# The head of a mixture-of-experts kernel: loads in halves, and the second half of the tokens turned by VectorE

## The chip, the cores and the metric

One NeuronCore of a Trainium2 chip runs the kernel. The metric is the device time of one execution in microseconds (us). All times below are in us, counted in the trace from the start of the profiled span.

## The reference

The input x has 8 sequences of 128 tokens, D = 128. Eight routed experts and one shared expert, each with F = 512, are applied to all tokens; nothing is skipped, the gates only weigh.

```
g = einsum('bsd,edf->ebsf', x, Wg);  u = einsum('bsd,edf->ebsf', x, Wu)      # E = 8
expert_outs   = einsum('ebsf,efd->ebsd', silu(g) * u, Wd)
expert_output = einsum('be,ebsd->bsd', gates, expert_outs)                   # gates: fside_Bx8_0
shared        = einsum('bsf,fd->bsd', silu(x @ Sg) * (x @ Su), Sd)
out = x + (1 - sg) * expert_output + sg * shared                             # sg: one number per sequence
```

## The kernel before, in words

**Layout.** The 1024 tokens are two halves of N = 512. A half is held transposed, features on the 128 partitions and tokens in the free dimension (`x_t`), in an order in which token 4p + q of the half is column 128q + p. A "unit" is one slice of 128 of the 512 hidden features of one expert for one half: 4 slices x 2 halves = 8 units per expert, 72 in all. All matmuls run in FP32R on values that are split in a high part (the rounded copy, `hi`) and the rest (`lo = whole - hi`); a product takes three matmuls (hi x hi, hi x lo, lo x hi) of 128x128 weights against 512 columns. A unit is nine matmuls: three for the gate (`g_ps`), three for up (`u_ps`), three for down (`y_ps`), the down ones two units late (LAG = 2).

**What follows a unit's matmuls.** ScalarE takes silu of g_ps (`silu_of`), VectorE multiplies it with u_ps into a bank of PSUM (`hidden`, L380), ScalarE makes the high part of that (`hidden_hi`, L303), VectorE the low part (`hidden_lo`, L385); then TensorE can do the down matmuls of the unit, that with h_lo last (L464). Two banks each for g, u and h: unit k's gate matmuls wait for silu k-2, its up matmuls for product k-2. Each engine runs its own list of instructions strictly in order; what stands behind a waiting instruction on its engine waits too. `.then_inc` and `wait_ge` are the semaphores between them.

**The head.** SyncE's queue issues, in this order: x first half, Sg, Su, x second half, Sd, the shared gate broadcast to 128 partitions, the gates broadcast to 128 partitions, then Wg, Wu, Wd of routed expert 1. TensorE does warm-up matmuls on zeros until the first half of x is there, and transposes it (L472). ScalarE and VectorE split it and the first weights (`first_hi`, L357, L273), VectorE and GpSimd the low parts. Then TensorE does the gate and up matmuls of the first two units (L483 to L502), turns the second half of x (four transposes, L508) and goes on to the units 3 to 8 of the shared expert (L519 to L529). VectorE does, in order: split of GATE 0:2, x_lo of the first half (L367), split of UP 2:4, split of DOWN (L357), products one and two (L380), first h_lo (L385), x_lo of the second half (L398), `not_sg` (L401) and `coef` = gates x (1 - sg) (L405), and from then on product, h_lo, product, h_lo. ScalarE takes the high part of the second half of x (L285) between the first and the second `hidden_hi`.

**Preparing the routed experts.** For each of them GpSimd scales x by coef (`xs`, L237; before the first expert it also adds hi and lo back to `x_t`, L224), ScalarE and GpSimd split xs and the weights, slice by slice, between their other work; for expert 1 ScalarE's first slice (L293) comes behind the third silu and needs all three of that expert's loads. Routed experts run in loops of the same pattern until a tail of transposes and stores that the change doesn't touch. In that tail the first half's result is turned by VectorE in 32x32 blocks (L432) and stored by four DMAs of 64 KB in rows of 128 B (L190).

Of the kernel before, what the change touches and what calls it, by code (L numbers as in the profile page):

```python
# [8 lines left out]
ALU = mybir.AluOpType  # L9
# [11 lines left out]
WARM_UP = 5  # L21


def build(nc, x, gates, shared_gate, Wg, Wu, Wd, Sg, Su, Sd, out):
# [21 lines left out]
    with ctx:  # L46
# [6 lines left out]
        x_nat = sbuf("x_nat", [P, HALVES, NQ, D], FP32)  # L53
# [41 lines left out]
        x_loaded = [sem(f"x_loaded{h}") for h in range(HALVES)]  # L95
        sg_loaded = sem("sg_loaded")
        gates_loaded = sem("gates_loaded")
        first_w_loaded = [sem(f"first_w_loaded{k}") for k in range(3)]
# [4 lines left out]
        one_minus = sem("one_minus")  # L103
        coef_ready = sem("coef_ready")
# [3 lines left out]
        x_t_done = sem("x_t_done")  # L108
        first_act_hi = sem("first_act_hi")
# [46 lines left out]

        @block.sync
        def _(sp):
            sp.dma_start(x_nat[:, 0, :, :], x_view[0]).then_inc(x_loaded[0], DMA)
            sp.dma_start(w_raw[0][:, GATE, :, :], in_slices(Sg)).then_inc(first_w_loaded[GATE], DMA)  # L160
            sp.dma_start(w_raw[0][:, UP, :, :], in_slices(Su)).then_inc(first_w_loaded[UP], DMA)
            sp.dma_start(x_nat[:, 1, :, :], x_view[1]).then_inc(x_loaded[1], DMA)
            sp.dma_start(w_raw[0][:, DOWN, :, :], in_rows(Sd)).then_inc(first_w_loaded[DOWN], DMA)
# [6 lines left out]
            sp.dma_start(sg_sb[:, :], shared_gate.partition_broadcast(P)).then_inc(sg_loaded, DMA)  # L170
            sp.dma_start(gates_sb[:, :, :], gates.partition_broadcast(P)).then_inc(gates_loaded, DMA)
# [28 lines left out]
        def _(pool):  # L200
# [19 lines left out]
            def whole_tokens(h):  # L220

                pool.wait_ge(x_hi_done, h + 2)
                pool.wait_ge(x_lo_done, h + 2)
                pool.tensor_tensor(x_t[:, h, :], f32(x_hi[:, h, :]), f32(x_lo[:, h, :]), ALU.add)\  # L224
                    .then_inc(x_t_done, 1)

            def prepare(e, buf, halves_before, slices_before, first=False):
                for h in range(HALVES):
                    if first:
                        whole_tokens(h)  # L230
                        pool.wait_ge(x_t_done, h + 1)
# [35 lines left out]
        def _(act):  # L267
            act.wait_ge(zeros_set, 1)
            act.activation(table[:, :], zeros[:, 0:1], ACT.Silu)

            def first_hi(k, n, m):
                act.wait_ge(first_w_loaded[k], DMA)
                act.activation(w_hi[0][:, k, n:m, :], w_raw[0][:, k, n:m, :], ACT.Copy)\  # L273
                   .then_inc(first_act_hi, 1)

            for i in range(2):
                act.wait_ge(x_transposed, i + 1)
                act.activation(x_hi[:, 0, i * HALF_N:(i + 1) * HALF_N], first_ps[i][:, 0:HALF_N], ACT.Copy)\
                   .then_inc(x_hi_done, 1)
# [73 lines left out]
        def _(dve):  # L353
            dve.memset(zeros[:, :], 0.0).then_inc(zeros_set, 1)

            def first_hi(k, n, m):
                dve.tensor_copy(w_hi[0][:, k, n:m, :], w_raw[0][:, k, n:m, :]).then_inc(first_dve_hi, 1)  # L357

            dve.wait_ge(first_w_loaded[GATE], DMA)
# [3 lines left out]
                              f32(w_hi[0][:, GATE, 0:2, :]), ALU.subtract).then_inc(first_dve_lo, 1)  # L363
            for i in range(2):
# [80 lines left out]
        def _(pe):  # L445
            def warm(cols):
                pe.matmul(u_ps[1][:, 0:cols], zeros[:, 0:P], zeros[:, 0:cols], start=True, stop=True)
# [21 lines left out]
            pe.wait_ge(x_loaded[0], DMA)  # L469
            for i in range(2):  # L470
                for q in range(HALF_Q):
                    last = pe.transpose(first_ps[i][:, q * P:(q + 1) * P], x_nat[:, 0, i * HALF_Q + q, :],  # L472
                                        ident[:, :])
                last.then_inc(x_transposed, 1)
            warm(HALF_N)
# [9 lines left out]
            pe.wait_ge(first_dve_lo, 1)  # L485
            for f in range(BANKS):
                pe.matmul(g_ps[f][:, :], w_lo[0][:, GATE, f, :], x_hi[:, 0, :], start=False, stop=False,
                          skip_group_check=True)
# [4 lines left out]
            pe.wait_ge(first_act_hi, 2)  # L493
# [6 lines left out]
            pe.wait_ge(first_pool_lo, 2)  # L500
# [3 lines left out]


            pe.wait_ge(x_loaded[1], DMA)
            for q in range(NQ):
                last = pe.transpose(y_ps[1][:, q * P:(q + 1) * P], x_nat[:, 1, q, :], ident[:, :])  # L508
            last.then_inc(x_transposed, 1)

            for k in range(BANKS, UNITS):
                f, h = k % NF, k // NF
                g, u = g_ps[k % BANKS], u_ps[k % BANKS]
                if k == NF:
                    pe.wait_ge(x_hi_done, 3)
                    pe.wait_ge(x_lo_done, 3)
                pe.wait_ge(silu_done, k - BANKS + 1)
                pe.wait_ge(first_act_hi, 1)
                pe.matmul(g[:, :], w_hi[0][:, GATE, f, :], x_hi[:, h, :], start=True, stop=False)  # L519
                pe.matmul(g[:, :], w_hi[0][:, GATE, f, :], x_lo[:, h, :], start=False, stop=False)  # L520
                pe.wait_ge(first_pool_lo, 1)
                pe.matmul(g[:, :], w_lo[0][:, GATE, f, :], x_hi[:, h, :], start=False, stop=True)\  # L522
# [9 lines left out]
                pe.wait_ge(first_pool_lo, 4 if k == BANKS else 5)  # L532
                down(k - LAG, k - LAG, 0, begin=(k - LAG) % NF == 0)
# [82 lines left out]
```

## Time and profile before

| | us |
|---|---|
| median of three runs (lowest, highest) | 158.86 (158.67, 158.95) |
| the profiled execution's own time | 158.84 |
| its span, first to last instruction | 157.0 |
| TensorE busy | 153.0 |
| VectorE, ScalarE, GpSimd busy | 99.2, 108.2, 78.5 |
| ScalarE: table load ends, first x_hi starts, first silu starts | 2.03, 4.26, 6.74 |
| GpSimd: first sum x_t, first xs start | 11.37, 12.75 |
| TensorE: the four transposes of the second half of x | 8.13 to 8.48 |

Busy time of TensorE is modelled: a matmul of 512 columns shows 0.389 us, but the next one starts 0.227 later, so starts are what one should subtract. "DMA" in the chain means that an instruction waited for a transfer.

### The profile page before, as it was taken

Reading aid. Unit: us, or ns where it says so; the run is one execution under the profiler, and the core shown is the slowest. Engines: PE = TensorE matmul, PEld = TensorE weight load, DVE = VectorE, ACT = ScalarE, POOL = GpSimd, SP = SyncE. Lnnn points to the kernel's source line nnn. Section 1 sums busy time; section 2 is a strip of 40 time slices with the busy share of each in tenths; the row PEclk is TensorE's granted clock in tenths of the full one; section 3 lists DMA queues with packets and bytes.
Section 4 is the critical chain, followed back from the end, with each engine's and each line's share of the span. In section 5 each row is a group of like instructions: output and inputs, shape, how many; then the busy total and the mean of one; then the engine's idle time right before and its main releaser. Section 6 shows DMA issues by size and latency. Waiting matters only on the chain.

```text
span 157.0 us, 2316 instructions
## 1 busy us (share of the span) xinstructions
PE 153.0 (97%) x674; PEld 124.8 (79%) x674; DVE 99.2 (63%) x160; ACT 108.2 (69%) x200; POOL 78.5 (50%) x79
## 2 busy tenths in 40 slices
PE   6999999999999999999999999999999999999992
PEld 2886888888888888888888888888888888888872
DVE  0695767766666666666666666666665666666782
ACT  3658767877577757775887667766776688755531
POOL 1549993556455464547255825573547354650000
DMA  5584014003300140006000600060000000000005
GB/s 157 187 265 136 0 49 156 0 0 104 100 0 0 39 168 0 0 14 186 0 0 0 200 0 0 0 199 1 0 0 0 0 0 0 0 0 4 0 10 124
DMA packets 10326, 8.24 MB, mean 52 GB/s; under 512 B 2896, under 2 KB 7760, under 8 KB 10320
## 3 DMA queue, kind: packets, MB, share of 16 engines
q1 hardware_dynamic: 10176, 8.03, 17.0%
q10 hardware_dynamic: 144, 0.13, 0.3%
q8 instruction: 3, 0.05, 0.1%
q14 instruction: 3, 0.02, 0.0%
HBM read 7.64 MB, written 0.52 MB: 52 GB/s over the span
## 4 chain that ended last, share of the span: by engine, by line
PE 89%; DMA 4%; SPq 2%; ACT 1%; DVE 1%; issue 0%
PE y_ps L464 10%; PE y_ps L461 10%; PE y_ps L459 10%; PE u_ps L551 9%; PE g_ps L546 9%; PE g_ps L547 9%; PE u_ps L552 9%; PE u_ps L550 9%; PE g_ps L545 9%; DMA w_raw<-in_L_cond_Wd 4%; DVE h_ps L380 0%; PE g_ps L520 0%; PE u_ps L526 0%; PE u_ps L527 0%; PE g_ps L522 0%; PE g_ps L519 0%
## 5 line engine op out<-in xcount | busy, mean ns | idle before, releaser
L380 DVE TENSOR_TENSOR h_ps<-silu,u_ps 128x512 f32<-128x512 f32 x71 | 49.4, 696 | 49.0 <-PE u_ps L552 45.6
L303 ACT ACTIVATE h_hi<-h_ps 128x512 fp32r<-128x512 f32 x71 | 42.6, 600 | 38.8 <-DVE h_ps L380 38.8
L242 POOL TENSOR_TENSOR w_lo<-w_raw,w_hi 128x384 fp32r<-128x384 f32 x32 | 32.5, 1019 | 37.7 <-ACT w_hi L293 37.7
L385 DVE TENSOR_TENSOR h_lo<-h_ps,h_hi 128x512 fp32r<-128x512 f32 x71 | 48.5, 683 | 0.1
L298 ACT ACTIVATE silu<-g_ps 128x512 f32<-128x512 f32 x72 | 42.9, 597 | 0.4 <-PE g_ps L491 0.4
L247 POOL TENSOR_TENSOR xs_lo<-xs,xs_hi 128x512 fp32r<-128x512 f32 x16 | 20.7, 1292 | 16.1 <-ACT xs_hi L289 16.1
L464 PE MATMUL y_ps<-h_lo,w_hi 128*128 128x512 f32 x71 | 27.9, 392 | 0.1
L459 PE MATMUL y_ps<-h_hi,w_lo 128*128 128x512 f32 x71 | 27.6, 389 | 0.0
L461 PE MATMUL y_ps<-h_hi,w_hi 128*128 128x512 f32 x71 | 27.6, 389 | 0.0
L545 PE MATMUL g_ps<-x_hi,w_hi 128*128 128x512 f32 x64 | 24.9, 389 | 0.0
L546 PE MATMUL g_ps<-x_lo,w_hi 128*128 128x512 f32 x64 | 24.9, 389 | 0.0
L547 PE MATMUL g_ps<-x_hi,w_lo 128*128 128x512 f32 x64 | 24.9, 389 | 0.0
L550 PE MATMUL u_ps<-xs_hi,w_hi 128*128 128x512 f32 x64 | 24.9, 389 | 0.0
L551 PE MATMUL u_ps<-xs_lo,w_hi 128*128 128x512 f32 x64 | 24.9, 389 | 0.0
L552 PE MATMUL u_ps<-xs_hi,w_lo 128*128 128x512 f32 x64 | 24.9, 389 | 0.0
L293 ACT ACTIVATE w_hi<-w_raw 128x384 fp32r<-128x384 f32 x32 | 16.6, 517 | 1.1 <-DMA w_raw<-in_L_cond_Wd 1.1
L237 POOL TENSOR_TENSOR xs<-x_t,coef 128x512 f32<-128x512 f32 x16 | 16.4, 1045 | 0.2
L464 PEld LDWEIGHTS y_ps<-h_lo,w_hi 128*128 128x128 f32 x71 | 13.3, 188 | 3.6 <-DVE h_lo L385 0.8
L459 PEld LDWEIGHTS y_ps<-h_hi,w_lo 128*128 128x128 f32 x71 | 13.3, 188 | 2.8
L461 PEld LDWEIGHTS y_ps<-h_hi,w_hi 128*128 128x128 f32 x71 | 13.3, 188 | 2.8
L545 PEld LDWEIGHTS g_ps<-x_hi,w_hi 128*128 128x128 f32 x64 | 12.0, 188 | 2.5
L550 PEld LDWEIGHTS u_ps<-xs_hi,w_hi 128*128 128x128 f32 x64 | 12.0, 188 | 2.5
(80 smaller groups left out, 119.8 us busy)
## 6 DMA issues: line engine op xcount, KB each, us to landing
w_raw<-in_L_cond_Wg SPq DMA_DIRECT2D x8, 256.0 KB, 2.7
w_raw<-in_L_cond_Wu SPq DMA_DIRECT2D x8, 256.0 KB, 3.1
w_raw<-in_L_cond_Wd SPq DMA_DIRECT2D x8, 256.0 KB, 3.6
x_nat<-in_x SPq DMA_DIRECT2D x2, 256.0 KB, 3.5
w_raw<-in_L_cond_Sg SPq DMA_DIRECT2D x1, 256.0 KB, 2.8
w_raw<-in_L_cond_Su SPq DMA_DIRECT2D x1, 256.0 KB, 4.2
w_raw<-in_L_cond_Sd SPq DMA_DIRECT2D x1, 256.0 KB, 4.7
out<-y_blk SPq DMA_DIRECT2D x4, 64.0 KB, 2.2
```

The lines of the kernel that those rows point to most:

```text
L298: act.activation(silu[k % BANKS][:, :], g_ps[k % BANKS][:, :], ACT.Silu)\
L303: act.activation(h_hi[k % HB][:, :], h_ps[k % BANKS][:, :], ACT.Copy)\
L380: dve.tensor_tensor((to or h_ps[k % BANKS])[:, :], silu[k % BANKS][:, :], u_ps[k % BANKS][:, :], ALU.mult).then_inc(hidden_done, 1)
L385: dve.tensor_tensor(h_lo[k % HB][:, :], h_ps[k % BANKS][:, :], f32(h_hi[k % HB][:, :]), ALU.subtract).then_inc(h_lo_done, 1)
L459: pe.matmul(y_ps[h][:, :], lo, h_hi[k % HB][:, :], start=begin, stop=False, skip_group_check=True)
L461: pe.matmul(y_ps[h][:, :], hi, h_hi[k % HB][:, :], start=False, stop=False, skip_group_check=True)
L464: pe.matmul(y_ps[h][:, :], hi, h_lo[k % HB][:, :], start=False, stop=f == NF - 1, skip_group_check=True)\
L545: pe.matmul(g[:, :], hi, x_hi[:, h, :], start=True, stop=False)
L546: pe.matmul(g[:, :], hi, x_lo[:, h, :], start=False, stop=False)
L547: pe.matmul(g[:, :], lo, x_hi[:, h, :], start=False, stop=True).then_inc(gate_done, 1)
L550: pe.matmul(u[:, :], hi, xs_hi[buf][:, h, :], start=True, stop=False)
L551: pe.matmul(u[:, :], hi, xs_lo[buf][:, h, :], start=False, stop=False)
```

## The change

- The loads of x's first half, Sg and Su are each split in two; UP's first half is split and multiplied before GATE's second half on ScalarE and GpSimd.
- The shared gate and the gates are loaded to one partition, by ScalarE's queue; VectorE computes one row of 72 coefficients there, TensorE spreads it to 128 partitions with a matmul against ones, VectorE copies it to `coef`.
- The second half of x is no longer loaded in rows of 2 KB and transposed by TensorE. It comes in four loads of 64 KB, each of 512 rows of 128 B, two issued by ScalarE's queue, two by SyncE's behind Sd; VectorE turns it in 32x32 blocks with one instruction ahead of the first product, into `x_t`, which the high part (ScalarE) and the low part (now GpSimd) are taken from.
- `x_t` of the first half is copied from PSUM by ScalarE, ahead of its first silu.
- Gate matmuls of the later units use w_lo before x_lo. Fewer warm-up matmuls at the start, three of 256 columns between the two halves of the first transposes.

The diff, cut to its core:

```diff
--- before.py
+++ after.py
@@ constants
-WARM_UP = 5
+WARM_UP = 4
+WARM_BETWEEN = 3
@@ tensors
-        x_nat = sbuf("x_nat", [P, HALVES, NQ, D], FP32)
+        x_nat = sbuf("x_nat", [P, NQ, D], FP32)
+        x_blk = sbuf("x_blk", [P, N], FP32)
...
-        gates_sb = sbuf("gates_sb", [P, B, E], FP32)
-        sg_sb = sbuf("sg_sb", [P, B], FP32)
-        not_sg = sbuf("not_sg", [P, B], FP32)
-        coef = sbuf("coef", [P, E, B], FP32)
+        gates_row = sbuf("gates_row", [1, B, E], FP32)
+        not_sg = sbuf("not_sg", [1, B], FP32)
+        row = sbuf("row", [1, E + 1, B], FP32)
+        ones = sbuf("ones", [1, P], FP32)
+        coef = sbuf("coef", [P, E + 1, B], FP32)
-        zeros = sbuf("zeros", [P, N], BF16)
+        zeros = sbuf("zeros", [P, P], BF16)
@@ loads
+        def load_blocks(queue, c):
+            of = x_view[1][:, :, c * BLK:(c + 1) * BLK].rearrange("(s j) q d -> j q s d", j=BLK)
+            queue.dma_start(x_blk[c * BLK:(c + 1) * BLK, :].rearrange("j (q s d) -> j q s d", q=NQ, d=BLK), of)\
+                 .then_inc(second_x_loaded, DMA)
@@ SyncE
-            sp.dma_start(x_nat[:, 0, :, :], x_view[0]).then_inc(x_loaded[0], DMA)
-            sp.dma_start(w_raw[0][:, GATE, :, :], in_slices(Sg)).then_inc(first_w_loaded[GATE], DMA)
-            sp.dma_start(w_raw[0][:, UP, :, :], in_slices(Su)).then_inc(first_w_loaded[UP], DMA)
-            sp.dma_start(x_nat[:, 1, :, :], x_view[1]).then_inc(x_loaded[1], DMA)
-            sp.dma_start(w_raw[0][:, DOWN, :, :], in_rows(Sd)).then_inc(first_w_loaded[DOWN], DMA)
+            load_tokens(0)
+            load_slices(GATE, Sg, 0)
+            load_tokens(1)
+            load_slices(GATE, Sg, 1)
+            load_slices(UP, Su, 0)
+            load_slices(UP, Su, 1)
+            sp.dma_start(w_raw[0][:, DOWN, :, :], in_rows(Sd)).then_inc(first_down_loaded, DMA)
+            load_blocks(sp, 2)
+            load_blocks(sp, 3)
...
-            sp.dma_start(sg_sb[:, :], shared_gate.partition_broadcast(P)).then_inc(sg_loaded, DMA)
-            sp.dma_start(gates_sb[:, :, :], gates.partition_broadcast(P)).then_inc(gates_loaded, DMA)
@@ GpSimd
             pool.wait_ge(first_act_hi, 1)
+            first_lo(UP, 0, 2)
+            pool.wait_ge(first_act_hi, 2)
             first_lo(GATE, 2, 4)
-            pool.wait_ge(first_act_hi, 2)
-            first_lo(UP, 0, 2)
...
-            def whole_tokens(h):
...
+            def second_x_lo():
+                pool.wait_ge(x1_hi_done, 1)
+                pool.tensor_tensor(x_lo[:, 1, :], x_t[:, 1, :], f32(x_hi[:, 1, :]), ALU.subtract)\
+                    .then_inc(x1_lo_done, 1)
@@ ScalarE
+            act.dma_start(row[:, E, :], shared_gate.partition_broadcast(1)).then_inc(sg_loaded, DMA)
+            act.dma_start(gates_row[:, :, :], gates.partition_broadcast(1)).then_inc(gates_loaded, DMA)
             act.wait_ge(zeros_set, 1)
             act.activation(table[:, :], zeros[:, 0:1], ACT.Silu)
+            load_blocks(act, 0)
+            load_blocks(act, 1)
...
+            def first_x_t(i):
+                act.wait_ge(x_lo_done, i + 1)
+                act.activation(x_t[:, 0, i * HALF_N:(i + 1) * HALF_N], first_ps[i][:, 0:HALF_N], ACT.Copy)\
+                   .then_inc(x_t_done, 1)
+            first_hi(UP, 0, 2)
             first_hi(GATE, 2, 4)
-            first_hi(UP, 0, 2)
+            first_x_t(0)
+            first_x_t(1)
             def second_x_hi():
-                act.wait_ge(x_transposed, 3)
-                act.activation(x_hi[:, 1, :], y_ps[1][:, :], ACT.Copy).then_inc(x_hi_done, 1)
+                act.wait_ge(x1_turned, 1)
+                act.activation(x_hi[:, 1, :], x_t[:, 1, :], ACT.Copy).then_inc(x1_hi_done, 1)
...
+            second_x_hi()
             hidden_hi(0, 0)
-            second_x_hi()
             hidden_hi(1, 1)
@@ VectorE
+            dve.memset(ones[:, :], 1.0).then_inc(ones_set, 1)
+            dve.wait_ge(sg_loaded, DMA)
+            dve.tensor_scalar(not_sg[:, :], row[:, E, :], -1.0, 1.0, ALU.mult, ALU.add)\
+               .then_inc(one_minus, 1)
...
+            dve.wait_ge(gates_loaded, DMA)
+            dve.wait_ge(one_minus, 1)
+            dve.tensor_tensor(row[:, 0:E, :].rearrange("p e b -> p b e"), gates_row[:, :, :],
+                              not_sg[:, :].unsqueeze(2).to_broadcast([1, B, E]), ALU.mult)\
+               .then_inc(row_ready, 1)
...
+            dve.wait_ge(row_spread, 1)
+            dve.tensor_copy(coef[:, :, :], y_ps[1][:, 0:(E + 1) * B].rearrange("p (e b) -> p e b", b=B))\
+               .then_inc(coef_ready, 1)
             first_hi(DOWN, 0, 4)
...
+            dve.wait_ge(second_x_loaded, DMA * (P // BLK))
+            dve.transpose(x_t[:, 1, :], x_blk[:, :]).then_inc(x1_turned, 1)
+            dve.wait_ge(x_t_done, 2)
             hidden(0, 0, first=True)
             hidden(1, 1, first=True)
             hidden_lo(0, 0)
-            dve.wait_ge(x_hi_done, 3)
-            dve.tensor_tensor(x_lo[:, 1, :], y_ps[1][:, :], f32(x_hi[:, 1, :]), ALU.subtract)\
-               .then_inc(x_lo_done, 1)
...
@@ TensorE
             for i in range(2):
+                pe.wait_ge(first_x_loaded[i], DMA)
...
-            warm(HALF_N)
+                if i == 0:
+                    for _ in range(WARM_BETWEEN):
+                        warm(HALF_N)
...
+            pe.wait_ge(ones_set, 1)
+            pe.wait_ge(row_ready, 1)
+            pe.matmul(y_ps[1][:, 0:(E + 1) * B], ones[:, :], row[:, :, :].rearrange("p e b -> p (e b)"), start=True,
+                      stop=True).then_inc(row_spread, 1)
...
-            pe.wait_ge(x_loaded[1], DMA)
-            for q in range(NQ):
-                last = pe.transpose(y_ps[1][:, q * P:(q + 1) * P], x_nat[:, 1, q, :], ident[:, :])
-            last.then_inc(x_transposed, 1)
```

## Rows read from the trace of the kernel before

**Rows 1.** The page: busy us (share of the span) and instructions of each engine.

```profile
PE 153.0 (97%) x674; PEld 124.8 (79%) x674; DVE 99.2 (63%) x160; ACT 108.2 (69%) x200; POOL 78.5 (50%) x79
```

**Rows 2.** Timeline (start, duration, engine, line, operation; idle before and releaser), TensorE.

```profile
12.53 0.19 PEld L464 LDWEIGHTS y_ps<-h_lo,w_hi 128*128 128x128 f32 x1 [0.30 <-DVE h_lo L385]
...
14.92 0.19 PEld L464 LDWEIGHTS y_ps<-h_lo,w_hi 128*128 128x128 f32 x1 [0.49 <-DVE h_lo L385]
...
15.26 0.39 PE L519 MATMUL g_ps<-x_hi,w_hi 128*128 128x512 f32 x1
...
149.92 0.39 PE L545 MATMUL g_ps<-x_hi,w_hi 128*128 128x512 f32 x1
```

**Rows 3.** Chain of waits in order of time (start, duration, what).

```profile
12.04 0.53 ACT w_hi L293
```

**Rows 4.** Timeline, VectorE in the head.

```profile
7.33 0.75 DVE L357 CAST w_hi<-w_raw 128x512 fp32r<-128x512 f32 x1 [1.00 <-DMA w_raw<-in_L_cond_Sd]
...
8.18 1.29 DVE L380 TENSOR_TENSOR h_ps<-silu,u_ps 128x512 f32<-128x512 f32 x2
...
10.14 0.68 DVE L398 TENSOR_TENSOR x_lo<-y_ps,x_hi 128x512 fp32r<-128x512 f32 x1
...
11.01 0.28 DVE L405 TENSOR_TENSOR coef<-gates_sb,not_sg 128x64 f32<-128x64 f32 x1
...
11.15 0.73 DVE L380 TENSOR_TENSOR h_ps<-silu,u_ps 128x512 f32<-128x512 f32 x1
```

**Rows 5.** Timeline, VectorE's turn of the result in the tail.

```profile
150.70 0.70 DVE L432 STREAM_TRANSPOSE y_blk<-y_t 128x512 f32<-128x512 f32 x1
...
151.33 0.65 DVE L385 TENSOR_TENSOR h_lo<-h_ps,h_hi 128x512 fp32r<-128x512 f32 x1
```

**Rows 6.** Timeline, ScalarE in the head.

```profile
8.91 0.60 ACT L303 ACTIVATE h_hi<-h_ps 128x512 fp32r<-128x512 f32 x1 [1.08 <-DVE h_ps L380]
...
9.40 0.59 ACT L285 ACTIVATE x_hi<-y_ps 128x512 fp32r<-128x512 f32 x1
```

**Rows 7.** Timeline, SyncE's first issues.

```profile
1.21 0.42 SPq L160 DMA_DIRECT2D w_raw<-in_L_cond_Sg  x1
...
1.66 0.43 SPq L161 DMA_DIRECT2D w_raw<-in_L_cond_Su  x1
...
2.14 0.43 SPq L162 DMA_DIRECT2D x_nat<-in_x  x1
```

**Rows 8.** DMA issues of 1.5 to 3.5: size each, us from issue to landing.

```profile
w_raw<-in_L_cond_Sg SPq DMA_DIRECT2D x1, 256.0 KB, 2.8
w_raw<-in_L_cond_Su SPq DMA_DIRECT2D x1, 256.0 KB, 4.2
x_nat<-in_x SPq DMA_DIRECT2D x1, 256.0 KB, 4.4
w_raw<-in_L_cond_Sd SPq DMA_DIRECT2D x1, 256.0 KB, 4.7
```

**Rows 9.** DMA rate from 0 to 20, forty steps of 0.5.

```profile
GB/s 0 0 0 57 233 324 377 287 242 264 326 313 136 76 20 77 216 279 366 334 237 143 301 339 367 335 185 10 0 0 0 0 0 0 0 0 0 0 0 0
```

**Rows 10.** The tail: line 190's issues, DMA rate 153 to 154, SyncE's last store.

```profile
L190 SPq DMA_DIRECT2D out<-y_blk x4: 614/629/705, 151.4 to 153.5; - x4
...
DMA to landing us min/median/max: 2.2/2.2/2.3
...
GB/s 148 148 123 113 154 143 138 133 139 118 123 82 32 15 0 0 0 0 46 67 82 118 143 138 148 138 143 148 138 143 108 148 154 128 138 128 123 123 77 32
...
154.23 0.58 SPq L193 DMA_DIRECT2D out<-out_sb  x1
```

**Rows 11.** Timeline, TensorE's start: warm-up weight loads, one per matmul; first gate matmuls.

```profile
2.03 0.15 PEld L447 LDWEIGHTS u_ps<-zeros 128*128 128x128 bf16 x1 [0.28 <-issue]
...
2.45 0.15 PEld L447 LDWEIGHTS u_ps<-zeros 128*128 128x128 bf16 x1 [0.28 <-issue]
...
4.79 1.20 PE L483 MATMUL g_ps<-x_hi,w_hi 128*128 128x256 f32 x4
```

More of the change, by code:

```diff
@@ L93, in build @@
         nat_ps = [g_ps[1], u_ps[0], y_ps[0]]
-        x_loaded = [sem(f"x_loaded{h}") for h in range(HALVES)]
+        first_x_loaded = [sem(f"first_x_loaded{i}") for i in range(2)]
+        second_x_loaded = sem("second_x_loaded")
         sg_loaded = sem("sg_loaded")
         gates_loaded = sem("gates_loaded")
-        first_w_loaded = [sem(f"first_w_loaded{k}") for k in range(3)]
+        first_w_loaded = [[sem(f"first_w_loaded{k}_{i}") for i in range(2)] for k in (GATE, UP)]
+        first_down_loaded = sem("first_down_loaded")
         w_loaded = [sem(f"w_loaded{i}") for i in range(2)]
@@ L103, in build @@
         one_minus = sem("one_minus")
+        ones_set = sem("ones_set")
+        row_ready = sem("row_ready")
+        row_spread = sem("row_spread")
         coef_ready = sem("coef_ready")
@@ L108, in build @@
         x_t_done = sem("x_t_done")
+        x1_turned = sem("x1_turned")
+        x1_hi_done = sem("x1_hi_done")
+        x1_lo_done = sem("x1_lo_done")
         first_act_hi = sem("first_act_hi")
@@ L229, in prepare @@
                     if first:
[L230 to L231 removed]
+                        if h == 1:
+                            second_x_lo()
+                        pool.wait_ge(x_t_done, 2)
                     else:
@@ L354, in _ @@
             dve.memset(zeros[:, :], 0.0).then_inc(zeros_set, 1)
+            dve.memset(ones[:, :], 1.0).then_inc(ones_set, 1)
+            dve.wait_ge(sg_loaded, DMA)
+            dve.tensor_scalar(not_sg[:, :], row[:, E, :], -1.0, 1.0, ALU.mult, ALU.add)\
+               .then_inc(one_minus, 1)
             def first_hi(k, n, m):
                 dve.tensor_copy(w_hi[0][:, k, n:m, :], w_raw[0][:, k, n:m, :]).then_inc(first_dve_hi, 1)
-            dve.wait_ge(first_w_loaded[GATE], DMA)
+            dve.wait_ge(first_w_loaded[GATE][0], DMA)
             first_hi(GATE, 0, 2)
@@ L446, in warm @@
             def warm(cols):
-                pe.matmul(u_ps[1][:, 0:cols], zeros[:, 0:P], zeros[:, 0:cols], start=True, stop=True)
+                pe.matmul(u_ps[1][:, 0:cols], zeros[:, :],
+                          zeros[:, :].unsqueeze(1).to_broadcast([P, cols // P, P]), start=True, stop=True)
             pe.wait_ge(zeros_set, 1)
@@ L484, in _ @@
                               stop=False, skip_group_check=True)
[L485 to L488, printed above, removed]
+                pe.wait_ge(first_dve_lo, 1)
+                for f in range(BANKS):
+                    pe.matmul(g_ps[f][:, cols], w_lo[0][:, GATE, f, :], x_hi[:, 0, cols], start=False,
+                              stop=False, skip_group_check=True)
+            pe.wait_ge(ones_set, 1)
+            pe.wait_ge(row_ready, 1)
+            pe.matmul(y_ps[1][:, 0:(E + 1) * B], ones[:, :], row[:, :, :].rearrange("p e b -> p (e b)"), start=True,
+                      stop=True).then_inc(row_spread, 1)
             pe.wait_ge(x_lo_done, 2)
@@ L514, in _ @@
                 if k == NF:
-                    pe.wait_ge(x_hi_done, 3)
-                    pe.wait_ge(x_lo_done, 3)
+                    pe.wait_ge(x1_hi_done, 1)
                 pe.wait_ge(silu_done, k - BANKS + 1)
-                pe.wait_ge(first_act_hi, 1)
+                pe.wait_ge(first_act_hi, 2)
                 pe.matmul(g[:, :], w_hi[0][:, GATE, f, :], x_hi[:, h, :], start=True, stop=False)
-                pe.matmul(g[:, :], w_hi[0][:, GATE, f, :], x_lo[:, h, :], start=False, stop=False)
-                pe.wait_ge(first_pool_lo, 1)
-                pe.matmul(g[:, :], w_lo[0][:, GATE, f, :], x_hi[:, h, :], start=False, stop=True)\
+                pe.wait_ge(first_pool_lo, 2)
+                pe.matmul(g[:, :], w_lo[0][:, GATE, f, :], x_hi[:, h, :], start=False, stop=False)
+                if k == NF:
+                    pe.wait_ge(x1_lo_done, 1)
+                pe.matmul(g[:, :], w_hi[0][:, GATE, f, :], x_lo[:, h, :], start=False, stop=True)\
                   .then_inc(gate_done, 1)
```

37 lines of the change are left out of this document (17 added, 20 removed).

## The prediction

> **What bounds the kernel now.** The page first: TensorE is busy for 153.0 of 157.0 us [rows 1]. Then how even its stream is: the first gate matmul of the shared expert's sixth unit starts at 15.26, that of the last unit of all (66 units later) at 149.92, so a unit takes 134.66 / 66 = 2.040 us, nine matmuls at 0.227 [rows 2]. That leaves no stall behind 15.26 that this change could touch, and the tail is not edited. What the change does to the time is by how much it moves that 15.26.
>
> The chain of waits says what sets 15.26: ScalarE's first split of routed expert 1 starts at 12.04, when its last weights (Wd) have landed, and h_hi, silu, product and h_lo follow, up to the matmul that takes h_lo at 14.92 [rows 2, 3]. So one bound is the landing T of that Wd, plus 15.26 - 12.04 = 3.22. The timeline of VectorE shows the second: its split of the down weights starts at 7.33, when Sd lands, the first product of silu and up at 8.18, and, behind the first h_lo, x_lo of the second half and two gate operations fill 10.14 to 11.15, ahead of the third product [rows 4]. TensorE waits for h_lo twice: 0.3 us before 12.53, and 0.49 before 14.92, and the next gate matmul behind such a wait comes 0.34 later instead of 0.227 [rows 2].
>
> **The chain that the new order makes.** I call L the moment at which VectorE starts to turn the second half. The turn of 128x512 stands in the trace once, at 150.70, and what follows it at 151.33: 0.63 [rows 5]. First product at L+0.63, second at L+1.28 (the two took 1.29 together [rows 4]). ScalarE's h_hi starts 0.03 behind a product's end and takes 0.60: L+1.36 to 1.95. First h_lo L+1.98 to 2.66, TensorE's matmul on it at L+2.70; the fourth unit starts 0.34 later, at L+3.04. ScalarE goes at 0.48 from one instruction to the next [rows 6]: second h_hi L+1.96, third silu L+2.44 to 3.04. With x_lo and the gate operations gone from here, the third product runs L+3.08 to 3.78 and the second h_lo L+3.68 to 4.36. TensorE wants it at L+3.04 + 8 x 0.227 = L+4.86, so there is no stall; the fifth unit starts at L+5.09, wants the third h_lo at L+6.91 and has it at L+6.2; the sixth unit starts at L+7.13. Checked on the kernel before: its first product at 8.18 means L = 7.55, a fourth unit at 10.59 (the trace has 10.65) and a sixth at 14.68; the 0.58 up to 15.26 are mostly the two stalls. So the new sixth unit starts at the later of L + 7.13 and T + 3.22, and the change is even where L is 8.13: it gives back 0.58 and pays for whatever puts the first product behind 8.18.
>
> **What sets L.** VectorE must have done the split of the down weights (0.65 behind the landing of Sd, if the turn follows at the pitch of rows 5, 0.75 at most by its duration [rows 4]), and all four block loads must have landed.
>
> Issues. SP's stand 0.45 to 0.48 apart, 0.47 on average [rows 7]. After the change Sd is the seventh, at 0.75 + 6 x 0.47 = 3.6, SP's two blocks come at 4.0 and, because a transfer of 512 short rows took 0.61 to 0.71 to issue in the tail [rows 10], at 4.7, done by 5.3. Sg had 2.8 from issue to landing, the blocks of the tail 2.2 [rows 8, 10], so the issues alone would allow Sd at 6.4 and the blocks at 6.9. The queue's data decide, not the issues.
>
> Data. The rate climbs from 57 GB/s at 1.5 to 324 at 2.5 and stays at 240 to 380 until 6.0 [rows 9]. Summed, 1024 KB are through by 5.4 and 1211 KB by 6.0. Last byte and landing stand 0.4 to 1.3 apart: Sg is 512 KB, reached at 3.6, landed 1.21 + 2.8 = 4.0; Su 768 KB, 4.55, landed 1.66 + 4.2 = 5.86; x of the second half 1024 KB, 5.4, landed 2.14 + 4.4 = 6.5 [rows 7 to 9]. Ahead of and with Sd there will be 1024 KB again (x's first half, Sg, Su, Sd), but beside them ScalarE's two blocks of 512 rows of 128 B. What such a load costs the trace doesn't show; its nearest row is the store of the same blocks in the tail, where busy engines moved 138 to 148 GB/s [rows 10]: 64 KB in 0.44 us. The cheap bound is the rate of long rows, 330 GB/s, 0.20 us. The dear bound: the broadcasts of the two gate tensors, 256 rows of 32 and 256 B, hold the queue from 6.2 to 7.6 at rates down to 20 GB/s [rows 9], 1.4 us for 16 rows on each of 16 DMA engines, 88 ns a row; at that price all 2048 rows would take 11 us. The blocks read distinct addresses, as those of the tail, so I take 0.44 each.
>
> Then Sd has its last byte at 5.4 + 2 x 0.44 = 6.3 and lands between 6.7 and 7.6, mean 7.15: VectorE is free at 7.8. SP's blocks have theirs at 6.3 + 0.88 = 7.15 and land between 7.55 and 8.45, mean 8.0. L = 8.0, set by the blocks. At the cheap rate Sd lands at 5.4 + 0.4 + 0.85 = 6.65 and the blocks at 7.05: L = 7.3, set by the split; with the late end of both landings L = 8.45.
>
> Forecast: sixth unit at 8.0 + 7.13 = 15.13, 0.13 earlier. T: 768 KB behind the blocks at 330 GB/s end at 7.15 + 2.33 = 9.5, with 1.4 to landing 10.9 (before: from 7.6, through near 10.6, landed at 12.04); the issues, the last at 6.3, would allow less. T + 3.22 = 14.1 is not the bound: the 1.1 us that the removed broadcasts give to Wd is bought and not used.
>
> The Trainium skill, "DMA: Bandwidth & Descriptors", section "Why small descriptors are slow (HBM only)", puts a fixed 3 cycles beside the 32 B beats of each packet; at its 850 MHz that makes an estimate of 8.2 ns for 128 B, 0.26 us a block where the tail's row says 0.44. By the page L would be about 7.45 and the time 158.2, by the row 158.7. The trace does not agree for stores (138 to 148 GB/s where that rule gives 248) and shows no such load, so the row is kept.
>
> **Edits costed at nothing, and what covers them.**
> - Loads in halves, UP's first half ahead of GATE's second: the first half of x can land by 0.75 + 2.2 = 2.95, x_hi starts 0.7 behind. The gate matmuls then start near 4.2 instead of 4.79 [rows 11], still at the slow pitch of rows 11 (0.42 for 512 columns, 1.2 GHz; 0.227 is 2.4 GHz). They end at 6.1 to 6.6, the up ones at 7.5 to 8.0, the third unit's gate ones by 8.7: all before the first product ends, at L+1.36 = 9.4. TensorE gains 0.1 to 0.6 and hands it to that wait; queued behind it are the third unit's up matmuls and the first down, which are in the chain above.
> - Four transposes less on TensorE (0.35), one matmul on a single row more: same cover.
> - ScalarE: two gate issues (0.9) ahead of the table load, which then ends at 2.9 instead of 2.03, two block issues (1.3) beside or behind it, 4.5 at worst; gates done as now even then. Two copies x_t of 0.38 ahead of the first silu, which comes by 7.5 instead of 6.74; it is needed, done, at 8.6.
> - VectorE: the row product on one partition, before 4.7, in its wait for x_hi; the copy of coef (nearest: the gate product, 0.28 [rows 4]) between up and down split, free unless Su's second half lands after 6.9; then 0.1.
> - GpSimd: two sums x_t less, x_lo of the second half more, 1.30 each; it is ready by 12 and TensorE wants it at L+5.5 = 13.5.
>
> **Sum.** The profiled execution took 158.84 for its span of 157.0, the median of three is 158.86: one and the same. 158.84 - 0.13 = 158.7.
>
> **Rivals.**
> 1. The blocks are cheap and the split of the down weights decides: L = 7.3 to 7.7, time 158.84 - 0.83 to - 0.43, say 158.2. For it: up to 377 GB/s on long rows, and Sg landed only 0.4 behind its last byte. Against: the stores of the tail.
> 2. The other side: the block loads land late, and VectorE, whose products all stand behind them in order, holds the kernel; each 0.1 us of landing past 8.13 is 0.1 lost. Issues of SP and ScalarE that take turns at one generator of descriptors would do it: 2 x 0.45 + 2 x 0.63 = 2.2 us of ScalarE's between SP's bring the last block's issue to 6.9, its landing, by 2.2, to 9.1: 158.84 + 0.97 = 159.8. For it: SP's last store, beside ScalarE's, took 0.58 to issue where loads of as many rows take 0.43 [rows 10]. Against: nothing else in the trace has two queues at once. Short rows at twice the tail's price give L = 5.4 + 3.5 + 0.85 = 9.75 and 160.5, at the broadcasts' price 165 or more.
> 3. TensorE, waiting 0.8 us near 9, falls back to the pitch of 0.42: some 15 matmuls at 0.2 more each, 3 us, 161.8. No wait of the kernel before is over 0.5 once it has sped up, so the trace bears it neither out nor down.
> 4. It does not do what it says: T comes at 12.04 again and binds; the sixth unit stays at 15.26. 158.85.
>
> **Chances.** Forecast 0.42 (own range 158.4 to 159.1), rival 1 0.26, rival 2 0.24, rival 3 0.03, rival 4 0.05. 0.2% is 0.32 us, about what a measurement of this kernel can tell from no change. Faster by more: rival 1 and a third of the forecast's range, 0.40. Slower: rivals 2 and 3 and a tenth of the forecast, 0.31. Within: 0.29. The range reaches from L = 7.3 to L = 9.4 (rival 2 without its dearest prices): 158.0 to 160.1.
>
> **What would show it.** Right: the turn starts at 7.8 to 8.3, at once behind the last block's landing; the first product 0.63 later; no wait for h_lo after 11; the sixth unit at 15.0 to 15.3, and 2.040 a unit behind it; Wd of expert 1 lands before 11; the stretch of idle DMA near 7 is gone. Wrong: block loads at another price than 0.44 each (SP's pair against Sd), SP's issues further apart than 0.47 while ScalarE issues, a pitch of 0.42 after 9, or a sixth unit later than L + 7.13, which would be a wait that I missed.

## The result, and the profile after

The changed kernel takes 159.45 us (159.13 to 160.03), the kernel before, timed beside it, 158.90 (158.46 to 159.40): a ratio of 1.0033, interval 1.0020 to 1.0045. It is slower, by 0.5 us, where 158.7, a little faster, was forecast. The profiled execution took 159.45 for a span of 157.6.

The timeline of TensorE answers to [rows 2]: the fourth, fifth and sixth unit, and the last.

```profile
11.86 0.39 PE L571 MATMUL g_ps<-x_hi,w_hi 128*128 128x512 f32 x1
...
13.94 0.39 PE L571 MATMUL g_ps<-x_hi,w_hi 128*128 128x512 f32 x1
...
15.98 0.39 PE L571 MATMUL g_ps<-x_hi,w_hi 128*128 128x512 f32 x1
...
150.62 0.39 PE L605 MATMUL g_ps<-x_hi,w_hi 128*128 128x512 f32 x1
```

The sixth unit stands at 15.98 instead of 15.26, and (150.62 - 15.98) / 66 = 2.040 a unit follow, as before. The loss, 0.72, is in the head; the profiled executions differ by 0.61, since the tail here takes 0.1 less. This holds for all fourteen profiled executions of this document: the time is the start of the sixth unit plus 143.47 to 143.58. So a time without a profile can be read as an estimate of its sixth unit: time - 143.5.

VectorE's timeline answers to [rows 4], with the turn that stood in the tail alone in [rows 5]:

```profile
7.71 0.76 DVE L405 CAST w_hi<-w_raw 128x512 fp32r<-128x512 f32 x1 [0.68 <-DMA w_raw<-in_L_cond_Sd]
8.81 0.71 DVE L451 STREAM_TRANSPOSE x_t<-x_blk 128x512 f32<-128x512 f32 x1 [0.34 <-DMA x_blk<-in_x]
9.44 1.26 DVE L436 TENSOR_TENSOR h_ps<-silu,u_ps 128x512 f32<-128x512 f32 x2
10.77 0.69 DVE L441 TENSOR_TENSOR h_lo<-h_ps,h_hi 128x512 fp32r<-128x512 f32 x1
11.86 0.70 DVE L436 TENSOR_TENSOR h_ps<-silu,u_ps 128x512 f32<-128x512 f32 x1 [0.39 <-ACT silu L342]
```

L, the moment at which VectorE starts to turn the second half, is 8.81, and the chain of the prediction puts the sixth unit at 8.81 + 7.13 = 15.94. Sd landed at 7.71 (before: 7.33), the last block only as the turn started, and the first product, 0.63 behind, comes 1.26 later than before; 0.58 of it is given back by the two stalls that are gone. TensorE waits for that product once, and goes on at its old pace of 0.23:

```profile
10.16 0.50 PE L580 MATMUL u_ps<-x_hi,w_hi 128*128 128x512 f32 x1 [0.94 <-DVE h_ps L436]
10.50 0.39 PE L581 MATMUL u_ps<-x_lo,w_hi 128*128 128x512 f32 x1
```

SyncE's and ScalarE's issues, and what the queue moved (the row of [rows 9] again, steps of 0.5):

```profile
1.66 1.36 ACTq L175 DMA_DIRECT2D x_blk<-in_x  x2
...
2.63 1.13 SPq L186 DMA_DIRECT2D w_raw<-in_L_cond_Su  x2
...
3.81 0.43 SPq L194 DMA_DIRECT2D w_raw<-in_L_cond_Sd  x1
...
4.28 1.41 SPq L175 DMA_DIRECT2D x_blk<-in_x  x2
```

```profile
GB/s 0 0 0 53 263 215 224 227 263 320 240 183 289 225 113 259 245 285 363 280 138 12 0 115 295 352 190 332 272 16 0 0 0 0 0 0 0 0 0 0
```

By 6.0 it has moved 994 KB (the sum of the steps, halved) where before it had 1211. Most of the difference, 161 of 217 KB, arises from 2.5 to 4.0: 215, 224 and 227 GB/s where the kernel before had 324, 377 and 287. The second bound, T + 3.22 (T is the landing of Wd of expert 1), is out of the way: ScalarE's first split of expert 1 starts with no wait.

```profile
11.71 0.53 ACT L337 ACTIVATE w_hi<-w_raw 128x384 fp32r<-128x384 f32 x1
```

### The profile page after: what moved, and what is told of

The parts are those of the page before. It is cut to its first block, busy times and chain, and to the rows that moved or that the text cites. A ratio compares the mean times of both kernels' runs of the same rounds, so it can differ in the third digit from the quotient of the medians.

```text
span 157.6 us, 2328 instructions
## 1 busy us (share of the span) xinstructions
PE 152.8 (97%) x675; PEld 124.2 (79%) x675; DVE 99.3 (63%) x162; ACT 109.1 (69%) x202; POOL 77.3 (49%) x78
## 4 chain that ended last, share of the span: by engine, by line
PE 92%; SPq 3%; DMA 2%; issue 1%; DVE 0%; ACT 0%; DVEq 0%
PE y_ps L514 10%; PE y_ps L511 10%; PE y_ps L509 10%; PE u_ps L611 9%; PE u_ps L610 9%; PE g_ps L606 9%; PE g_ps L605 9%; PE u_ps L612 9%; PE g_ps L607 9%; DMA x_blk<-in_x 2%; SPq L186 1%; PE u_ps L580 1%; PE u_ps L583 1%; PE u_ps L581 1%; PE g_ps L573 1%; PE g_ps L576 1%
## 5 line engine op out<-in xcount | busy, mean ns | idle before, releaser
L607 PEld LDWEIGHTS g_ps<-x_hi,w_lo 128*128 128x128 f32 x64 | 12.0, 188 | 2.5
```

Of the source, the lines that this page charges most:

```text
L607: pe.matmul(g[:, :], lo, x_hi[:, h, :], start=False, stop=True).then_inc(gate_done, 1)
```

## Experiments

Theory A: the place of the turn is the loss. Theory B: the loads in halves and the blocks delay what VectorE waits for. Later, for what delays the loads: theory C says that the halves slow the queue, rival D that it is ScalarE's two block loads ahead of Sd. Each result is the median, then its ratio to the kernel before on the same chip with the interval. The diffs are cut to their core, some calls shortened. One execution of each kernel was profiled, and it need not stand for the median.

**1. The turn behind the first h_lo.**

```diff
-dve.wait_ge(second_x_loaded, ...); dve.transpose(x_t[:, 1, :], x_blk[:, :])
 hidden(0, 0, first=True); hidden(1, 1, first=True); hidden_lo(0, 0)
+dve.wait_ge(second_x_loaded, ...); dve.transpose(x_t[:, 1, :], x_blk[:, :])
-second_x_hi()            # ScalarE, ahead of hidden_hi(0)
+second_x_hi()            # ScalarE, behind silu_of(2)
```

> The changed kernel with one thing moved: VectorE turns the second half behind the first h_lo instead of ahead of the first product, and ScalarE takes its high part behind the third silu. Loads and all else as changed. Theory A (the turn's place: all products stand behind the last block's landing, and the sixth unit of the changed kernel is L + 7.13 with L = 8.81): the first product now waits only for the split of the down weights, from 8.81 + 0.63 = 9.44 back to 7.71 + 0.70 = 8.4; the turn runs near 10.4, the third product waits for it until 11.0, the third h_lo is ready at 14.4 and wanted at 14.7, the sixth unit starts at 14.9 to 15.0 instead of 15.98: about 158.4 to 158.5 where the changed kernel takes 159.45. Theory B (the loads in halves and the blocks on the queues delay Su and Sd, the place is indifferent): the first product stays behind 9 and the time within 0.3 of the changed kernel.

158.71, 0.9988 (0.9970 to 1.0006): 0.45% below the changed kernel, whose interval it doesn't touch. VectorE:

```profile
7.76 0.54 DVE L406 CAST w_hi<-w_raw 128x512 fp32r<-128x512 f32 x1 [0.20 <-DMA w_raw<-in_L_cond_Sd]
8.41 1.29 DVE L437 TENSOR_TENSOR h_ps<-silu,u_ps 128x512 f32<-128x512 f32 x2
9.78 0.69 DVE L442 TENSOR_TENSOR h_lo<-h_ps,h_hi 128x512 fp32r<-128x512 f32 x1
10.38 0.70 DVE L456 STREAM_TRANSPOSE x_t<-x_blk 128x512 f32<-128x512 f32 x1
11.01 0.67 DVE L437 TENSOR_TENSOR h_ps<-silu,u_ps 128x512 f32<-128x512 f32 x1
```

The loads are as late as in the changed kernel, but the first product is 1.03 earlier and the sixth unit stands at 15.01. Theory A holds. The forecast of 158.4 to 158.5 is met by the profiled execution (158.48), and missed by the median.

**2. Block loads with long rows.** The same bytes, 4 rows of 512 B to a partition; the tokens of the second half are then not in their places.

```diff
-of = x_view[1][:, :, c * BLK:(c + 1) * BLK].rearrange("(s j) q d -> j q s d", j=BLK)
+of = x_view[1][c * BLK:(c + 1) * BLK, :, :]
```

> The changed kernel with its four block loads reading long rows: the same four transfers of 64 KB to the same 32 partitions each, but 4 rows of 512 B to a partition instead of 16 rows of 128 B (what is turned is then not the second half's tokens in their right places). Theory A with the price of short rows as the mis-sized term: SyncE issues them 0.47 apart instead of 0.70, they take 0.2 instead of 0.44 or more of the queue each, Sd lands at 7.1 to 7.3 instead of 7.71 and the last block at 7.7 or before instead of 8.79; the turn then waits for the split of the down weights and starts at 7.8 to 8.0, sixth unit at 15.0 to 15.1, time 158.5 to 158.6. Rival (not the rows but the number of transfers and bytes ahead of them sets L): last block at 8.4 or later, time 159.1 or more.

Its times scatter from 159.3 to 161.9, so only its trace (159.28) is read. The issues are shorter, but Sd still lands at 7.79, and the turn now waits for the split and not for a block:

```profile
7.79 0.93 DVE L405 CAST w_hi<-w_raw 128x512 fp32r<-128x512 f32 x1 [1.14 <-DMA w_raw<-in_L_cond_Sd]
8.64 0.70 DVE L451 STREAM_TRANSPOSE x_t<-x_blk 128x512 f32<-128x512 f32 x1
```

SyncE's blocks took 3.1 from issue to landing, so the last was there near 8.0, some 0.8 before that of the changed kernel (8.79; I had worked out 4 x 0.24 = 0.96, and 0.2 of the 0.8 is an earlier issue). Sd, behind ScalarE's two blocks, gained nothing from their long rows, where the price of 0.44 instead of 0.20 for each would have given it 0.5. So short rows don't explain Sd, and their price isn't settled by this run. Sixth unit 15.78, and 8.64 + 7.13 = 15.77. The forecast of L near 8.0 missed.

**3. The first part alone** (halves, gate rows; the second half in 2 KB rows and through TensorE, as before).

```diff
-load_blocks(sp, 2); load_blocks(sp, 3)      # and both of ScalarE
+sp.dma_start(x_nat1[:, :, :], x_view[1])    # ahead of Sd
-dve.transpose(x_t[:, 1, :], x_blk[:, :])   # x_lo by VectorE behind the first h_lo, as before
...
+for q in range(NQ): pe.transpose(y_ps[1][:, q * P:(q + 1) * P], x_nat1[:, q, :], ident[:, :])
```

> Only the first part of the change: x's first half, Sg and Su in halves, gate rows on one partition and spread by TensorE, x_t of the first half by ScalarE. The second half comes as before in rows of 2 KB ahead of Sd, is transposed by TensorE, split by ScalarE and VectorE where the kernel before has it. Theory A (only the turned second half costs): first product at 8.2 to 8.4, no gate operations between x_lo and the third product, Wd of expert 1 landed by 11, the sixth unit at 14.7 to 14.9 instead of 15.26 before: 158.3 to 158.5, the 0.5 of stalls of before won. Theory B (halves and gate rows cost, since SyncE issues two transfers more ahead of Sd): Su and Sd land 0.3 to 0.5 later than before, first product at 8.6 or later, time equal to before or slower.

158.76, 0.9987 (0.9974 to 1.0000). This is B's side: the time is not told from that of before, Sd landed at 7.93, 0.6 later than before, and the first product started at 8.87, 0.69 later. A's 158.4 missed. What the product waited for were not the loads, though, but the up matmuls:

```profile
8.87 1.29 DVE L428 TENSOR_TENSOR h_ps<-silu,u_ps 128x512 f32<-128x512 f32 x2 [0.51 <-PE u_ps L553]
```

**4. The gate rows alone**, all loads whole and in their old order (the diff is against the kernel before).

```diff
-sp.dma_start(sg_sb[:, :], shared_gate.partition_broadcast(P)); sp.dma_start(gates_sb[:, :, :], ...)
+act.dma_start(row[:, E, :], shared_gate.partition_broadcast(1)); act.dma_start(gates_row[:, :, :], ...)
+pe.matmul(y_ps[1][:, 0:(E + 1) * B], ones[:, :], row, start=True, stop=True)
...                                                     # row product and copy of coef by VectorE
```

> The kernel before with the gate tensors alone changed: both loaded to one partition by ScalarE's queue, row of 72 coefficients spread by one matmul and copied by VectorE. All other loads whole and in their old order. Both theories: the dead stretch of the DMA queue from 6.2 to 7.6 goes and Wd of expert 1 lands at 10.5 to 10.9 instead of 12.0; the two gate operations leave the place between x_lo and the third product. By the two bounds the sixth unit is at 7.55 + 7.13 = 14.7 to 14.8: 158.3 to 158.4. If instead the landing of Wd stays near 12, the broadcasts were not what held the queue, and the time stays within 0.1 of before.

158.78, 0.9988 (0.9969 to 1.0007). The dead stretch of the queue is gone, as forecast, and it has moved 1233 KB by 6.0; the time is not the 158.3 to 158.4 forecast. TensorE says why, in the head:

```profile
6.17 0.44 PE L500 MATMUL y_ps<-row,ones 1*128 1x72 f32 x2
6.54 0.73 PE L504 MATMUL g_ps<-x_lo,w_hi 128*128 128x512 f32 x2
7.11 0.62 PE L508 MATMUL u_ps<-x_hi,w_hi 128*128 128x512 f32 x2
```

The spread matmul, on one row and 72 columns, holds TensorE for 0.37; what it delays are the up matmuls that the first product waits for (8.53 instead of 8.18). I had costed it at nothing. In experiment 3 the same 0.37 is about half of the 0.69; the other half is not accounted for.

**5. The changed kernel with whole loads** of x's first half, Sg and Su.

```diff
-load_tokens(0); load_slices(GATE, Sg, 0); load_tokens(1); load_slices(GATE, Sg, 1)
-load_slices(UP, Su, 0); load_slices(UP, Su, 1)
+sp.dma_start(x_nat[:, :, :], x_view[0])               # warm-up matmuls as in the kernel before
+sp.dma_start(w_raw[0][:, GATE, :, :], in_slices(Sg)); sp.dma_start(w_raw[0][:, UP, :, :], in_slices(Su))
```

> The changed kernel with x's first half, Sg and Su loaded whole again (three transfers of 256 KB instead of six of 128 KB, warm-up matmuls as before); blocks, gate rows and the turn's place as changed. Theory C (the halves slow the queue: 994 KB through by 6.0 in the changed kernel, 1021 with long block rows, 995 in the kernel without blocks, against 1211 before and 1233 with gate rows alone): 1150 KB or more by 6.0, Sd lands at 7.0 to 7.3 instead of 7.71, the last block 0.6 to 0.9 earlier, 7.9 to 8.2, so L = 7.9 to 8.2 and the sixth unit at 15.0 to 15.4 instead of 15.98: 158.7 to 158.9. Rival D (ScalarE's blocks ahead of Sd are what slows it): Sd stays at 7.6 or later, L at 8.6 or later, 159.3 or more.

159.28, 1.0018 (0.9997 to 1.0038). The interval overlaps that of the changed kernel (1.0020 to 1.0045), so in time no gain is shown, and the median is rival D's side. The profiled execution has C's side, but it is the third fastest of twelve (158.76):

```profile
7.22 0.74 DVE L394 CAST w_hi<-w_raw 128x512 fp32r<-128x512 f32 x1 [0.43 <-DMA w_raw<-in_L_cond_Sd]
8.07 0.71 DVE L440 STREAM_TRANSPOSE x_t<-x_blk 128x512 f32<-128x512 f32 x1
```

```profile
GB/s 0 0 0 33 70 377 406 324 303 188 287 291 235 296 330 342 350 278 84 3 0 4 135 287 389 337 333 81 7 0 0 0 0 0 0 0 0 0 0 0
```

1140 KB by 6.0; L = 8.07, sixth unit 15.24 (8.07 + 7.13 = 15.20). The median of 159.28 stands for a sixth unit near 15.78, so an L near 8.65, against the 8.81 of the changed kernel, whose profiled execution took the median time. These two are estimates by time - 143.5 and L + 7.13.

**6. All blocks by SyncE, behind Sd**, loads in halves.

```diff
-load_blocks(act, 0); load_blocks(act, 1)
+load_blocks(sp, 0); load_blocks(sp, 1)     # ahead of load_blocks(sp, 2)
```

> The changed kernel with all four block loads issued by SyncE behind Sd, none by ScalarE; loads still in halves. Rival D (ScalarE's two blocks, 128 KB ahead of Sd, and their issues beside SyncE's, delay Sd): Su's second half is issued at 3.1 and Sd at 3.56 instead of 3.81, Sd lands at 7.0 to 7.2. Theory C (halves): Sd gains 0.2 from the issue and some 0.3 from the bytes at most, 7.3 or later. By both the last block lands later than 8.79, since SyncE needs 2 x 0.68 us more to issue: at 9.4 to 9.8; the chain is L + 7.13, so 16.5 to 16.9 and 160.0 to 160.4.

159.79, 1.0057 (1.0036 to 1.0078), 0.2 below its forecast. Sd landed early, at 6.84, as rival D has it, and VectorE waited longer for the blocks:

```profile
6.84 0.82 DVE L405 CAST w_hi<-w_raw 128x512 fp32r<-128x512 f32 x1 [0.25 <-DMA w_raw<-in_L_cond_Sd]
8.96 0.71 DVE L451 STREAM_TRANSPOSE x_t<-x_blk 128x512 f32<-128x512 f32 x1 [1.30 <-DMA x_blk<-in_x]
```

Sixth unit 16.12 (8.96 + 7.13 = 16.09). Here and in the changed kernel the last block sets L, in 2 and 5 the split of the down weights; the last block was 0.5 earlier than I expected. Rival D is not shown by the early Sd: in experiment 9, with the same issues, Sd landed at 7.71.

**7 and 8. Late turn with whole loads; then the spread matmul behind the first up matmuls too**, its copy behind the turn. 7 is the edits of 1 and 5; 8 adds:

```diff
-pe.matmul(y_ps[1][:, 0:(E + 1) * B], ones, row, ...)    # ahead of w_hi GATE x x_lo
 up matmuls of the units 1 and 2
+pe.matmul(y_ps[1][:, 0:(E + 1) * B], ones, row, ...)
-dve.tensor_copy(coef, y_ps[1])                          # ahead of the split of DOWN
 dve.transpose(x_t[:, 1, :], x_blk[:, :])
+dve.tensor_copy(coef, y_ps[1])
```

> Turn behind the first h_lo and whole loads together, spread matmul where the change has it, between the two halves of the gate matmuls. By the sum of both: Sd at 7.1 to 7.3, so VectorE could start the first product at 8.0; but the gate matmuls start at 4.8 as before and the spread matmul holds TensorE 0.37 us (6.07 to 6.44 in the changed kernel), so the up matmuls end at 8.5 and the first product starts there, as it did at 8.53 with gate rows alone: sixth unit at 15.0 to 15.1, 158.5 to 158.6. If the spread matmul costs nothing, first product at 8.0 to 8.2 and 158.2.

> As the one with the turn behind the first h_lo and whole loads, and the spread matmul moved behind the up matmuls of the first two units, its copy to coef behind the turn. TensorE then ends the first up product at 8.15 as before, first product 8.15 to 8.2; the spread takes its 0.37 where the four transposes stood (0.35). L' = 8.18 - 0.63 = 7.55, fourth unit at 10.6, the copy (0.15 to 0.23) delays the third product to 11.0 and the second h_lo to 12.3, wanted at 12.4; sixth unit at 14.7 to 14.8: 158.3, 0.3% below the kernel before. If the copy and the turn together are too much for VectorE, a wait for h_lo of 0.1 to 0.3 appears near 12.4 or 14.5 and the time is that of the kernel with the spread in place.

158.88, 1.0006 (0.9988 to 1.0024), and 159.01, 1.0006 (0.9991 to 1.0021): both medians missed. The profiled execution of 7, its fastest (158.50, sixth unit 14.99), is as forecast; Sd landed at 7.62 and the first product started at 8.41. With whole loads the late turn is thus no faster than with halves (158.71 in experiment 1). In 8 the first product started at 8.49, still behind the up matmuls, and coef came late (copy at 11.08). GpSimd's program has its first xs, which needs coef, ahead of x_lo of the second half; that x_lo ended at 13.65 and TensorE waited 0.40 for it: the sixth unit stands at 15.42. A copy moved out of one wait went into another.

```profile
11.36 1.04 POOL L257 TENSOR_TENSOR xs<-x_t,coef 128x512 f32<-128x512 f32 x1 [1.22 <-DVE coef L444]
12.36 1.29 POOL L242 TENSOR_TENSOR x_lo<-x_t,x_hi 128x512 fp32r<-128x512 f32 x1
```

**9 to 12. Late turn put together with the rest.** 9: all blocks by SyncE. 10: as 9, the spread matmul behind the up matmuls, its copy ahead of the turn. 11: as 10, two of the blocks by ScalarE between its first copies. 12: as 10, whole loads.

```diff
 hidden_lo(0, 0)
+dve.tensor_copy(coef, y_ps[1])                          # 10, 11, 12
 dve.transpose(x_t[:, 1, :], x_blk[:, :])
 act.activation(x_hi[:, 0, ...], first_ps[i][:, 0:HALF_N], ACT.Copy)
+load_blocks(act, i)                                     # 11 alone
```

> The changed kernel with two things moved: the turn behind the first h_lo, and all four block loads issued by SyncE behind Sd. With the blocks behind, Sd landed at 6.84 instead of 7.71 and the up matmuls ended at 8.2; with the turn late, nothing of VectorE's head waits for the blocks, which landed at 8.96 there and are wanted at 10.0. First product at 8.2, where the up matmuls end, L' = 7.57, sixth unit at 14.7 to 14.8; the landing T of Wd of expert 1, issued at 8.0 with 3.6 to 4.0 to go, 11.6 to 12.0, gives T + 3.22 = 14.8 to 15.2 as the second bound: 158.3 to 158.7. Should T not bind, 158.3; if the time is that of the late turn alone (158.7), T or the up matmuls took over.

> As the one with the turn late and all blocks by SyncE behind Sd, and the spread matmul moved behind the first up matmuls, its copy between the first h_lo and the turn. The up matmuls end 0.37 earlier, 7.83; the split of the down weights at 7.6; first product 7.85, L' = 7.2, so 14.4 by the first bound, but T + 3.22 stays at 14.8 to 15.2 by the second: 158.3 to 158.7, no better than with the spread in place. If it is 158.0, T was not what held it.

> As the one before it, but two blocks issued by ScalarE between its first copies x_hi (at 3.8 and 4.9, behind most of the shared expert's bytes), two by SyncE behind Sd. SyncE then issues Wd of expert 1 at 6.7 to 6.9, T at 10.7 to 11.2, T + 3.22 at 14.4 at most; Sd lands at 7.0 to 7.3, first product at 7.9 to 8.1, sixth unit at 14.5 to 14.7: 158.0 to 158.3, below both kernels. If ScalarE's issues (0.66 each) delay its x_hi of the second quarter or its split of the up weights by more than 0.3, the up matmuls end at 8.3 and it is 158.5.

> The kernel with the turn late, four block loads by SyncE behind Sd and the spread matmul behind the up matmuls (158.48, the best so far), now with x's first half, Sg and Su loaded whole. If the halves cost the queue what the sums by 6.0 say (922 to 1045 KB in all eight kernels with halves, 1126 to 1233 in the five with whole loads), Sd lands at 7.2 to 7.4 instead of 7.77 and the sum by 6.0 is over 1120 KB; but the first gate weights then land at 4.2 instead of 3.4 and TensorE ends its up matmuls of the first unit near 8.3, which takes the place of the split as what the first product waits for: first product 8.3 to 8.5, sixth unit 14.9 to 15.1, time within 0.15 of 158.5. If it is 158.2 or less, the landing of Sd was the whole bound; if 158.8 or more, the early start of the gate matmuls in the halved kernels was worth more than the queue.

9: 158.88, 0.9996 (0.9979 to 1.0014), 0.2 above its forecast. 10: 158.48, 0.9965 (0.9952 to 0.9978), as forecast. 11: 158.52, 0.9973 (0.9957 to 0.9989), where 158.0 to 158.3 was forecast: Sd landed at 8.11 and not at 7.0 to 7.3, the first product started at 8.78. 12: 158.59, 0.9976 (0.9956 to 0.9996), as forecast: with the queue faster (Sd at 7.45), the up matmuls are what the first product waits for.

```profile
7.45 0.43 DVE L395 CAST w_hi<-w_raw 128x512 fp32r<-128x512 f32 x1 [0.85 <-DMA w_raw<-in_L_cond_Sd]
8.52 1.30 DVE L423 TENSOR_TENSOR h_ps<-silu,u_ps 128x512 f32<-128x512 f32 x2 [0.65 <-PE u_ps L544]
```

Versions 10, 11 and 12 beat both kernels, 12 only just beyond its interval; between them no difference is shown, so here too whole loads (12) gain nothing on halves (10). The gain of 10 over 9 (0.3%) is more than the traces account for. The profiled execution of 10 is its slowest run (158.83, sixth unit 15.34), that of 9 one of its faster ones (158.53, sixth unit 15.06). What in 10's faster runs is earlier stays open.

## Why the prediction was wrong

- **The chain behind L was right.** With the turn ahead of all products the sixth unit is at L + 7.13: 15.94, 15.77, 15.20 and 16.09 worked out, 15.98, 15.78, 15.24 and 16.12 measured (the changed kernel, experiments 2, 5 and 6). So were: even at L = 8.13, 0.58 of stalls given back, T no bound, no wait for h_lo from the fourth unit on, 2.040 behind it, all as read from the kernel before.
- **The mis-sized term is L**, 8.0 forecast, 8.81 measured, past the late end of 8.45 that the sum gave. The time, 159.45, lies inside the outer range (158.0 to 160.1), on the side of rival 2, which had 0.24; the forecast had the wrong sign. The 0.81 are three parts. The first two make Sd, forecast at 7.15, landed at 7.71; the third is the last block behind it.
- **First part, 0.26: the bytes ahead of Sd.** The step that failed is "Ahead of and with Sd there will be 1024 KB again". I took the queue's rate from whole loads and put "loads in halves" under the edits costed at nothing. The sum has 1024 KB and two blocks, 1152 KB, through by 6.3. The trace has 1081 there and 1152 only at 6.56 (taking the bytes in order of issue, as the sum does). All kernels with halves had moved 922 to 1045 KB by 6.0, those with whole loads 1126 to 1233 (before, 4, 5, 7, 8, 12). That the queue moves fewer bytes with halves is shown by this; that the halves are what made the changed kernel slow is not, since 5, 7 and 12 gained nothing in time that is shown.
- **Second part, 0.30: from the last byte of Sd to its landing**, 7.71 - 6.56 = 1.15 where 0.85 was the mean. It is inside the 0.4 to 1.3 read before. Sd of one and the same order of loads landed at 6.84 and at 7.71 (experiments 6 and 9); why stays open.
- **Third part, 0.25: from Sd to the last block**, 1.1 instead of 0.85. SyncE's last block was issued at 5.07, not 4.7, since the second half of Su took 0.63 to issue, beside ScalarE's, and the first block 0.74. That is a small share of rival 2's shared issue. The price of 0.44 a block stays open (experiment 2). Rival 1, L of 7.3 to 7.7, did not come. The estimate from the Trainium skill, "DMA: Bandwidth & Descriptors", section "Why small descriptors are slow (HBM only)", 0.26 a block, would have put L at 7.45, further off. No run here separates it from 0.44.
- **The step "VectorE, whose products all stand behind them in order"** was costed properly, but the choice of place was what made late landings dear: with the turn behind the first h_lo, the same late landings cost 0.7 less (experiment 1). This is the one cause that the times show.
- **Costed at nothing and not nothing:** the spread matmul, 0.37 on TensorE. In the changed kernel L covers it (the wait for the product was 0.94 long). It took the gain of experiment 4 and part of that of 3.
- Gate matmuls started at 4.68 instead of 4.2 and the up ones ended near 8.4, not 8.0, since the second part of x's first half landed at 4.49. L covers this as well. Rival 3 did not come: TensorE waited 0.94 and went on at 0.23 a matmul.
- A rival that no run separates is inside "halves": the rows of 1 KB, or the issues. SyncE issues a load every 0.47, and 128 KB in 0.47 is 279 GB/s at most (worked out, not measured), less than the 324 and 377 that the queue reached with whole loads from 2.5 on. The prediction said "The queue's data decide, not the issues" and didn't work this out. In the changed kernel the rate was 215 to 227 there, below even that, so the issues alone don't account for it.

## What to carry to other kernels

Put a transfer's consumer, on an in-order engine, as late as its own consumer allows, not ahead of work that is ready: here the price of a late load was one for one. A load split in halves brings fewer bytes by a given time; count them in a trace of that shape before you cost the split at nothing. When one profiled execution shows a gain and the median doesn't, go by the median. A small operation on the bottleneck engine is free only while something else is later than it.

## What the runs showed of the hardware

- Six transfers of 128 KB in rows of 1 KB moved fewer bytes by 6.0 than three of 256 KB in rows of 2 KB, in every profiled kernel (922 to 1045 KB in eight, 1126 to 1233 in six; means 980 and 1164, 16% less). Most of it arises from 2.5 to 4.0. Whether it is the row or the number of transfers wasn't separated.
- With the same issues up to 6.8, at the same times to 0.01, Sd landed at 6.84, 7.71 and 7.77 in three profiled kernels (experiments 6, 9, 10). The landing scatters by almost 1 us from one execution to another, which is more than most of what is compared here; one profile a kernel shows a mechanism, not 0.3 us.
- A matmul with one row of weights and 72 columns in fp32 holds TensorE for 0.37, as long as 1.6 matmuls of 512 columns at full speed.
- The split of 128x512 on VectorE took 0.43 to 0.93 in different runs; why stays open.
